# FFN banks reused a step later, selections on GpSimd, low halves behind the state, weight work of tile 0 in two phases: one change to a GRU and mixture-of-experts kernel

## What is computed

```python
def cell(h, x):
    gi = x @ W_ih + b_ih
    gh = h @ W_hh + b_hh
    i_r, i_z, i_n = jnp.split(gi, 3, axis=-1)
    h_r, h_z, h_n = jnp.split(gh, 3, axis=-1)
    r = jax.nn.sigmoid(i_r + h_r)
    z = jax.nn.sigmoid(i_z + h_z)
    n = jnp.tanh(i_n + r * h_n)
    h_new = (1.0 - z) * n + z * h
    return (h_new, h_new)
...
scores = xf @ gate_w.T + gate_b + bias
top_scores, top_idx = jax.lax.top_k(scores, TOP_K)       # TOP_K = 2 of E = 8
gates = jax.nn.softmax(top_scores, axis=-1)
comb = jnp.sum(jax.nn.one_hot(top_idx, E, dtype=gates.dtype) * gates[..., None], axis=1)
h = jax.nn.silu(jnp.einsum('td,ehd->teh', xf, w1) + b1)  # H = 352
y = jnp.einsum('teh,edh->ted', h, w2) + b2
out = jnp.einsum('ted,te->td', y, comb)
```

## Time and profile before

| | us |
|---|---|
| median of 3 runs | 2164.16 (2162.59 to 2166.87) |
| the profiled execution | 2168.39 |
| its span, first to last instruction | 2166.6 |
| PE busy | 1972.8 (91%) |
| DVE busy | 1381.9 (64%) |
| ACT busy | 897.6 (41%) |
| POOL busy | 318.5 (15%) |

### The profile page before, as it was taken

The page is one execution under the profiler, slowest core; times in us unless marked ns, Lnnn a source line. Parts: engine busy times, 40 slices in busy tenths (PEclk is TensorE's granted clock), DMA queues, the critical chain, the costliest instruction groups (busy, mean ns, idle before and its releaser), DMA issues.

```text
span 2166.6 us, 80653 instructions
## 1 busy us (share of the span) xinstructions
PE 1972.8 (91%) x34348; PEld 1693.5 (78%) x34348; DVE 1381.9 (64%) x5702; ACT 897.6 (41%) x2894; POOL 318.5 (15%) x471
## 2 busy tenths in 40 slices
PE   5899999999998999886899999998998998999999
PEld 3677677677676889775798898897887987988988
DVE  5565666666666155677677677677676775776763
ACT  1355455455455233343343343343443433433433
POOL 0041231242111000241110110110110100100112
PEclk9999999999999999997999999899999998998999
DMA  8000000000001611111000000000000000000000
GB/s 316 1 1 1 1 1 1 1 1 1 1 1 59 216 61 52 51 45 34 3 18 18 21 11 18 27 4 28 18 5 25 18 18 13 18 18 12 4 12 11
DMA packets 53594, 63.19 MB, mean 29 GB/s; under 512 B 7377, under 2 KB 44113, under 8 KB 52209
## 3 DMA queue, kind: packets, MB, share of 16 engines
q1 hardware_dynamic: 53232, 58.02, 7.9%
HBM read 42.77 MB, written 15.24 MB: 27 GB/s over the span
## 4 chain that ended last, share of the span: by engine, by line
PE 41%; DVE 9%; issue 2%; ACT 1%; DVEq 0%; ACTq 0%
PE ps L1048 22%; PE ps L1492 9%; PE ps L1470 8%; DVE hp L1122 2%; ACT nn L1063 1%; DVE dh L1111 1%; DVE dh L1117 1%; DVE hn L1101 1%; DVE hn L1103 1%; DVE hn L1095 1%; DVE hn L1098 1%; PE ps L1481 1%; DVE hp L1125 1%; DVE ns L1113 1%; DVE h L1123 0%
## 5 line engine op out<-in xcount | busy, mean ns | idle before, releaser
L1048 PEld LDWEIGHTS ps<-hp,whf 128*128 128x128 f16 x24576 | 644.7, 96 | 111.7 <-DVE hp L1125 89.9
L1048 PE MATMUL ps<-hp,whf 128*128 128x32 f16 x24576 | 660.3, 177 | 73.4 <-DVE hp L1125 67.5
L1063 ACT ACTIVATE rz<-s,sc 128x32 f32<-128x32 f32 x512 | 164.6, 322 | 402.9 <-DVE s L1092 395.6
L1470 PE MATMUL ps<-hs,w1f 128*128 128x256 f16 x2112 | 285.4, 281 | 34.5 <-DVE wi L1671 34.5
L1492 PE MATMUL ps<-wi,w2f 128*128 128x256 f16 x2112 | 276.5, 279 | 0.0
L1591 POOL TENSOR_TENSOR wi<-wi 128x256 f16<-128x256 f32 x176 | 120.4, 689 | 1035.7 <-ACT wi L1571 1035.7
L1470 PEld LDWEIGHTS ps<-hs,w1f 128*128 128x128 f16 x2112 | 208.7, 101 | 72.3 <-DVE wi L1671 40.4
L1492 PEld LDWEIGHTS ps<-wi,w2f 128*128 128x128 f16 x2112 | 195.3, 99 | 27.2 <-issue 3.0
L1090 DVE TENSOR_TENSOR s<-ps,gi 128x32 f32<-128x32 f32 x256 | 48.6, 190 | 232.4 <-PE ps L1048 232.0
L1063 ACT ACTIVATE nn<-hn,sc 128x32 f32<-128x32 f32 x256 | 82.3, 322 | 240.8 <-DVE hn L1103 240.8
L1222 PE MATMUL ps<-x1T,wi 128*128 128x256 f32 x768 | 179.3, 391 | 1.0 <-PEq L440 1.0
(11 more groups left out here) (213 smaller groups left out, 3002.5 us busy)
## 6 DMA issues: line engine op xcount, KB each, us to landing
gi_d<-stage SPq DMA_DIRECT2D x84, 128.0 KB, 1.7
gi<-gi_d SPq DMA_DIRECT2D x14, 768.0 KB, 5.1
...
```

Source lines behind the costliest of these rows:

```text
L1048: last = nc.tensor.matmul(ps[:, bank, g * WIDE * 2 * B:(g + 1) * WIDE * 2 * B], w[:, k, q, g, a, :], moving, start=(k == 0 and a == 0), st ...
L1063: nc.scalar.activation(o.rearrange("p g b -> p (g b)"), i_.rearrange("p g b -> p (g b)"), func, scale=un).then_inc(done, 1)
L1470: last = nc.tensor.matmul(ps[:, 6 + i % 2, 0:TT], w1p[:, k, i // NC2, wp, (i % NC2) * P:(i % NC2 + 1) * P], hs[:, f % 2, k, hq, :, :].rear ...
```

## The change

1. Up products no longer share a step with the L1671 that frees their bank: from the third chunk on `room_for_ups` puts them at least one step behind it, and the table asserts `>` instead of `>=`. The other lists follow from it.
2. The selection matrices are built by GpSimd at the head of `other_tiles`, both 32-row blocks by one cast; `idh` and `combh` stay with DVE (`blank`).
3. GpSimd's subtraction waits, besides for its input, for the end of the state before its own step (`t.v_h`).
4. Weight work of tile 0: maxima of w1 in steps 0 to 5, its scale by step 8, its pieces in steps 9 to 16; maxima of w2 in steps 8 to 15, its scale by step 18, its pieces in steps 19 to 29. A piece a step; its cast stands one step behind ACT's scaling (`CASTS_AT`). b1 is loaded ahead of w2, b2 twice.
5. b2 becomes a pair of fp16 in `b2p`, built by GpSimd; a bias product is two fp16 matmuls with `gates` as the moving side, and the transposes and the eviction of `combT` go.

```diff
-    for _ in range(2 * NCH):
-        while load[s] >= 3 or at[-2:] == [s, s]:
+    for n in range(2 * NCH):
+        while load[s] >= 3 or at[-2:] == [s, s] or n >= 4 and s < at[(n - 4) | 1] + 2:
             s += 1
...
-MAXIMA_AT = [1 + j for j in range(16)]
-MAXIMA_DONE, SCALES_AT, SPLIT_FIRST = 17, 19, 20
+MAXIMA_AT = [0, 1, 1, 2, 3, 3, 4, 5, 8, 9, 10, 11, 12, 13, 14, 15]
+MAXIMA_DONE = [6, 16]
+SCALES_AT = [8, 18]
 NPIECES = 8 + NC2
-SPLIT_AT = [SPLIT_FIRST + j * (SPT - SPLIT_FIRST) // NPIECES for j in range(NPIECES)]
+SPLIT_AT = [9 + j for j in range(8)] + [19 + j for j in range(NC2)]
+CASTS_AT = [x + 1 for x in SPLIT_AT]
...
                     for j in range(NPIECES):
-                        if SPLIT_AT[j] == s:
+                        if CASTS_AT[j] == s:
...
-                sp.dma_start(b2[:, :], ins["b2"]).then_inc(d_s, 16)
+                for r in (0, 32):
+                    sp.dma_start(b2[r:r + NE, :], ins["b2"]).then_inc(d_s, 16)
...
-                    nc.tensor.matmul(ps[:, 4 + m // 2, (m % 2) * TT:(m % 2 + 1) * TT], b2[:, m * P:(m + 1) * P],
-                                     combT[:, :], start=(m % 2 == 0), stop=False, skip_group_check=True)
+                    for wp in range(2):
+                        nc.tensor.matmul(ps[:, 4 + m // 2, (m % 2) * TT:(m % 2 + 1) * TT], b2p[:, wp, m * P:(m + 1) * P],
+                                         gates[:, :], start=(m % 2 == 0 and wp == 0), stop=False,
+                                         skip_group_check=True)
...
+                nc.gpsimd.memset(b2p[:, :, :], 0.0)
+                nc.gpsimd.memset(selm[:, :, :], 0.0)
+                link(nc.gpsimd.tensor_tensor(either[:, :], ident[0:64, 0:NE], ident[0:64, 32:32 + NE], ALU.add))
+                for n, parts in enumerate(SELECTIONS):
+                    for e, p0, p1 in parts:
+                        last = nc.gpsimd.tensor_copy(selm[0:64, n, p0:p1],
+                                                     either[:, e:e + 1].broadcast_to((64, p1 - p0)))
+                link(last)
+                for r in (0, 32):
+                    link(nc.gpsimd.tensor_copy(b2p[r:r + NE, 0, :], b2[r:r + NE, :]))
+                    link(nc.gpsimd.tensor_tensor(b2p[r:r + NE, 1, :], b2[r:r + NE, :], b2p[r:r + NE, 0, :],
+                                                 ALU.subtract))
...
                             j = g * NCH + i
+                            if n < NT:
+
+                                pool.wait_ge(t.v_h, (n * SPT + s) * 4)
                             ready(pool, a_h, j + 1)
```

More of the change, by code:

```diff
@@ L950 @@
 for _i in range(NCH):
-    assert UP_AT[2 * _i] >= earlier(ACT_AT, _i, 2)
+    assert UP_AT[2 * _i] > earlier(ACT_AT, _i, 2)
     assert DOWN_AT[2 * _i] > REST_AT[_i]
@@ L1232, in _ @@
                     t.pe_step(s)
-                    if s == MAXIMA_DONE + 1:
-                        pe.wait_ge(v_a, S_BASE)
-                        for i in range(4):
-                            last = nc.tensor.transpose(ps[0:1, 7, i * P:(i + 1) * P], mxa[:, i:i + 1], ident)
-                        last.then_inc(p_a, 1)
-                    if s == SCALES_AT:
-                        pe.wait_ge(v_a, S_BASE + 1)
-                        nc.tensor.matmul(ps[:, 7, 0:4], ones1, mx1[:, :], start=True, stop=True)\
-                            .then_inc(p_a, 1)
+                    for phase in range(2):
+                        w = 4 if phase == 0 else 1
+                        if s == MAXIMA_DONE[phase] + 1:
+                            pe.wait_ge(v_m, 2 * phase + 1)
+                            for i in range(w):
+                                last = nc.tensor.transpose(ps[0:1, 7, i * P:(i + 1) * P], mxa[:, i:i + 1], ident)
+                            last.then_inc(p_a, 1)
+                        if s == SCALES_AT[phase]:
+                            pe.wait_ge(v_m, 2 * phase + 2)
+                            nc.tensor.matmul(ps[:, 7, 0:w], ones1, mx1[:, 0:w], start=True, stop=True)\
+                                .then_inc(p_a, 1)
                     for u in range(NQ, UNITS):
@@ L1302, in small_ones @@
                 def small_ones():
-                    dve.wait_ge(d_s, 16 * (4 + sum(len(segments(c)) for c in range(NCH))))
-                    step(nc.vector.tensor_tensor(gb[:, :], gb2[:, 0, :], gb2[:, 1, :], ALU.add))
-                    step(big(mx[:, 2, 0:1], gw[:, :, :]))
-                    step(big(mx[:, 3, 0:1], b1[:, :]))
+                    dve.wait_ge(d_s, 16 * (5 + sum(len(segments(c)) for c in range(NCH))))
+                    nc.vector.tensor_tensor(gb[:, :], gb2[:, 0, :], gb2[:, 1, :], ALU.add)
+                    big(mx[:, 1, 0:1], gw[:, :, :])
+                    big(mx[:, 2, 0:1], b1[:, :])
+                    step(big(mx[0:NE, 3, 0:1], b2[0:NE, :]))
                 def maxima(j):
@@ L1516, in ffn_slice @@
                         ready(pe, v_rt, (f + 1) * R_STEPS)
+                        ready(pe, v_sel, 1)
                         for g in range(2):
-                            nc.tensor.transpose(ps[0:NE, 3, g * P:(g + 1) * P], comb[:, g, :], ident)
-                        for g in range(2):
-                            last = nc.tensor.matmul(ps[:, 3, TT + g * P:TT + (g + 1) * P], combh[:, g, :], idh[:, :],
+                            last = nc.tensor.matmul(ps[:, 3, g * P:(g + 1) * P], combh[:, g, :], idh[:, :],
                                                     start=(g == 0), stop=True, skip_group_check=True)
@@ L1552, in ffn_slice @@
                         ready(act, p_ct, f + 1)
[L1553 to L1554 removed]
+                        nc.scalar.activation(gates[:, :], ps[:, 3, 0:TT], ACT.Copy).then_inc(a_gt, 1)
                     for n, g in due(CB_AT, s, f, now, late):
@@ L1595, in _, with blank @@
             def _(dve):
[L1596 removed]
+                def blank():
                     nc.vector.tensor_copy(idh[:, :], ident)
[L1598 to L1608 removed]
+                    nc.vector.memset(combh[:, :, :], 0.0).then_inc(v_sel, 1)
                 bc = lambda x: x.unsqueeze(2).broadcast_to((P, 2, NE))
@@ L1688, in _ @@
                         if n == 1 and s == 0:
-                            selections()
+                            blank()
                         ffn_slice(n - 1, s, n <= NT, n >= 2)
```

130 lines of the change are left out of this document (80 added, 50 removed).

## The result

The changed kernel takes 2058.07 us (median of four runs, 2057.46 to 2060.65) beside 2165.51 us for the kernel before in the same session (2162.59 to 2169.63): a ratio of 0.9505, 95% interval 0.9486 to 0.9523. That is 107.4 us less; 2065 us had been forecast (99 less), so the time came out 7 us better and within the range. The profiled execution took 2057.46 us, its span 2055.7. But two terms of the sum were far off, one each way, and three smaller ones by 4 to 5 us, and they largely made up for each other, as the experiments show.

A forecast was written before the change was run, and what follows sets the result against it. Tile 0 was taken as PE-bound, tiles 1 to 7 as a chain of 4.38 us a step with PE's load nearly as long. −29 −5 −19 −45.6 +2.6 −3 = −99 off the median 2164.16 gives 2065 us, range 2045 to 2093.

The forecast's parts named there:

- A: Tile 0's weight work: the 13 steps behind the first 16 lose 30.3 us, casts waiting on ACT; −29, bounds −30 and −20.
- stop in step 2: Tile 0: one more DMA, all ahead of the same gi_d stores, so the stop of some 8 us stays, give or take 1.
- B: First step of tile 1: selection casts leaving DVE save 9.3 us, GpSimd collisions give back 4; −5, bounds −9 and +2.
- C: Tiles 1 to 7: 48 stalls of 0.48 us at L1122 go, PE gives back 4 us; −19, bounds −23 and −10.
- D: Steps 8 to 11 of seven tiles: PE's bank wait and low clock go, 184.18 to 138.6 us; −45.6, bounds −59 and −29.
- E: Last gate moves into step 0 of the next tile, 0.42 us more before L1090; +2.6 us, bounds 0 and +6.
- F: fp16 b2 products: −1.4 us in the tiles, the rest in the last 76.5 us; together −3, bounds −1 and −6.
- (1): DVE becomes the bound: stretched gates, outputs and L1671 delay L1090 in more steps than 8 to 10; 2090 us, chance 0.15.
- (3): GpSimd holds DVE up where it used not to: B at +2, A at −20; 2081 us, chance 0.10.
- (4): Collisions stay because the state counter GpSimd waits for is met earlier: C at 0; 2084 us, chance 0.04.
- (5): Slower than before: PE waits for low halves at each of 154 chunks; at 1 us a chunk 2219 us, chance 0.02.
- (2): PE never waits in steps 8 to 11 and the clock stays at 2.4 GHz: D at −59; 2051 us, chance 0.12.

## Why the prediction was right, and where it was not

The terms beside what they measured; "undone" is what the changed kernel loses without the part, "alone" what the kernel before gains by it, in medians.

| part | forecast | undone | alone | by stretches |
|---|---|---|---|---|
| A, tile 0 (steps 3 to 31) | −29 | | | −27.8 |
| A, stop in step 2 | 0, give or take 1 | | | +5.3 |
| B, selections | −5 | −9.4 | | −9.6 |
| C, low halves | −19 | −23.0 | −19.1 | −20.9 |
| D, banks | −45.6 | −34.8 with E | −31.2 with E | |
| E, late gate | +2.6 | | | +2.3 |
| F, fp16 b2 | −3 | −18.6 | −17.7 | |

A and the stop by stretches and the others undone (E is in D undone) add up to −108.3, beside −107.4 measured: the parts are nearly independent, so each can be judged by itself.

**A** was right in size (+1.6 in the sixteen steps, −29.4 in the thirteen) and half wrong in cause: the wait on ACT was named with the two casts, and costs nothing at one piece a step without a maximum; the loss stood in the intervals with two pieces. **The stop** is the step that failed outright: "all ahead of the same gi_d stores, so the stop of some 8 us at step 2 stays, give or take 1" counted how many issues stand ahead of the store and not when their bytes move. The order of b1 and w2 is exactly what mattered; it cost 5.3 us.

**B**: the nine us that leave DVE were right (14.17 − 4.61 = 9.6). The 4 us of collisions were priced with casts of 0.37 us by a row of other shape; they take 0.21, and the state beside them stretches by 0.4 us at most. What does stretch it is b2's pair, 1.9 us, which belongs to F. The Trainium skill, "SBUF — State Buffer", Who interferes with whom, was used for the memsets, which only write. They ran almost wholly beside DVE operations that read PSUM with one SBUF input. The one with two that starts beside them (L1104 at 978.52, 0.13 us before the end of the memset at 977.06) lasts its usual 0.19 us: the trace agrees, on one short overlap. For the reading kind it agrees too: beside b2's casts and subtractions from 983.75 on, three operations with two SBUF inputs last 0.60 to 1.09 us.

**C**: right by its mechanism, 196 ns for the write where 192 was forecast. Of the 4 us given back to PE little shows: undone, tiles 1 to 7 lose 20.9 of the 21.5 us by which the writes lengthen. Alone, the median has the 19 of the forecast, but runs differ by as much as the 2 to 4 us in question.

**D and F** are the two terms most out of size. D charged the whole fall of steps 8 to 11 to the banks: 184.18 to 138.6, at 19.8 us a tile. Without fp16 b2 the changed kernel has 145.3 there, 20.8 a tile; the 19.8 assumed, in "b2 and the broadcast add 0.25 on PE", what only F brings. Two of its tiles, at a granted clock of 1.00, do take 19.6 us, since b2's price was too low (0.25 with the broadcast, where b2 alone takes 1.24 more than as fp16) by about as much as DVE's lateness was too high; the other five have the low clock. DVE's lateness: the intervals behind states 7 and 8 take 4.7 us each in tiles 3 to 6, 0.3 above the usual 4.38 where 0.5 and 1.2 were forecast. F was priced in the kernel before, where the f32 products lie behind bank waits, and "beside the chain" was taken to hold. It holds neither after the change, when PE is the limit there (8.7 us), nor before it: fp16 b2 alone took 20.3 us off these steps, with the granted clock at 0.93 in five tiles of seven where it had been at 0.93 in one. So a row's 487 ns per product was read, but not that stretches with these products have a lower granted clock. That the total came out within 9 us is in part luck: D with E was 8 to 12 us too large and the stop cost 5.3 more, against 15 more from F and 4 more each from B and C.

**The tail**: 76.5 before, 76.4 after, though F was to bring 2 us. With f32 b2 the changed kernel has 77.9, so F brings 1.5, and the rest of the change, by all signs the new table, takes 1.4 (with the old banks it is 75.3). PE's waits behind the last state of the changed kernel:

```profile
PE ps L1531 <- DVE x1T L1741: 1.6, 1, 1.6
PE ps L1558 <- ACT hs L1080: 0.8, 1, 0.8
PE ps L1570 <- DVE combh L1715: 0.8, 1, 0.8
PE ps L1518 <- DVE wi L1734: 0.7, 1, 0.7
```

They are 3.9 us, where before there were 3.1 (1.8 on L1671, 1.3 on ACT): "two bank waits shrink" came true (1.8 to 0.7), but b2's products now arrive ahead of the output addition that clears their banks, and the routing is waited for.

Of the rivals, (1), (3), (4) and (5) did not come: DVE did not become the bound, GpSimd's casts cost little, the mean of the write is 196 ns, and PE waits for no low half in any row of its waits. Rival (2) came nearly whole in steps 8 to 11: 55.3 us less at a granted clock near 1, where it had 59, but 16.3 of it by fp16 b2; the time lies midway between its 2051 and the 2065. The signs were met or passed: 196 ns, no wait of PE on L1734 (the L1671 of the changed file), 128.9 / 7 = 18.4 us for steps 8 to 11 where about 20 was named, tiles 2 to 7 at 142.7 to 143.7 us where 144 to 146 was, the first interval of tile 1 at 6.47 us where 9 was. Only tile 0 missed its sign: with the stop it is 22.5 us shorter where 29 was named. All bounds at their best, taken off the median, give 2164 − 127 = 2037 us and not 2041; nothing else hangs on it.
